# Keys and values turned in 64-row tiles, multiplied in 32-column tiles, and bias additions shared with ScalarE

## What is computed

```python
# L0: shifted windows of 8 x 8 pixels, 16 heads of 16 channels, one 64 x 64 matrix and a bias per head
y = einsum('nhjd,hij->nhid', windows(x), w) + b[None, :, :, None]
# L1: linear attention over all 4096 pixels, 64 heads of 8 channels
qkv = einsum('bchw,oc->bohw', x, w_qkv)
y = grouped_1x1(depthwise_5x5(qkv))
q, k, v = relu(q), relu(k), pad(v, ones)      # 32 heads from qkv, 32 from y
vk  = einsum('bhdn,bhen->bhde', v, k)         # 9 x 8 for each head
out = einsum('bhde,bhen->bhdn', vk, q);  out = out[:-1] / (out[-1:] + 1e-15)
out = batchnorm(einsum('bchw,oc->bohw', out, w_proj))
```

## Time and profile before

| | |
|---|---|
| median of three runs | 3008.99 us (3006.94 to 3009.3) |
| the profiled execution | 3003.14 us, its span 3001.5 us |
| mixing, until about | 450 us |
| projections, until about | 1300 us |
| heads, until about | 2410 us |
| output | the rest |
| granted TensorE clock, mean | 0.978 of 2.4 GHz |
| busy TensorE / VectorE / ScalarE / GpSimd | 91 / 74 / 48 / 29% |

### The profile page before, as it was taken

One profiled execution on the slowest core, in us unless ns is written; L12 is line 12 of the kernel. 1 busy time (PEld: TensorE's weight loads), 2 busy tenths in 40 slices (PEclk: granted clock), 3 DMA queues, 4 the chain that ended last, 5 costly groups with the idle time before them and its releaser, 6 DMA issues. The chain is left out here.

```text
span 3001.5 us, 46675 instructions
## 1 busy us (share of the span) xinstructions
PE 2742.5 (91%) x14847; PEld 2197.1 (73%) x14847; DVE 2230.3 (74%) x3385; ACT 1449.6 (48%) x1977; POOL 864.8 (29%) x1109
## 2 busy tenths in 40 slices
PE   4999979999989999879999999999999969999997
PEld 3777768878877888757777777777777836666665
DVE  5787875445445544389999999999999957777674
ACT  3434425444544544456566566566656523333332
POOL 6300004444444444500000000000000027777776
PEclk9999989999999999989999999999999989999999
DMA  4535336765766675655545555555555456776662
GB/s 152 211 148 208 146 114 208 233 225 191 231 218 218 203 235 181 205 155 134 133 128 134 134 130 132 136 131 131 137 131 131 122 196 243 260 266 241 238 238 112
DMA packets 285057, 534.16 MB, mean 178 GB/s; under 512 B 35184, under 2 KB 232560, under 8 KB 279280
## 3 DMA queue, kind: packets, MB, share of 16 engines
q1 hardware_dynamic: 274256, 468.11, 50.7%
q0 software_dynamic: 7936, 38.80, 3.7%
q10 hardware_dynamic: 2720, 25.43, 2.3%
HBM read 281.26 MB, written 254.15 MB: 178 GB/s over the span
## 5 line engine op out<-in xcount | busy, mean ns | idle before, releaser
L1565 POOL TENSOR_TENSOR ql<-q,qh 128x1024 fp32r<-128x1024 f32 x128 | 304.1, 2399 | 1180.2 <-ACT qh L1593 1180.2
L1213 PE MATMUL c_ps<-dh,wh 128*128 128x512 f32 x1152 | 476.4, 414 | 87.5 <-ACT m2s L1132 66.9
L1213 PE MATMUL c_ps<-dh,wl 128*128 128x512 f32 x1152 | 454.8, 395 | 0.0
L1213 PE MATMUL c_ps<-dl,wh 128*128 128x512 f32 x1152 | 454.5, 395 | 0.0
L1125 ACT ACTIVATE dh<-diff 128x1088 fp32r<-128x1088 f32 x192 | 213.7, 1113 | 431.4 <-DVE diff L1329 430.5
L837 PE MATMUL o_ps<-xh,wqh 128*128 128x512 f32 x768 | 327.6, 427 | 40.6 <-DVE xl L914 30.9
L1213 PEld LDWEIGHTS c_ps<-dh,wh 128*128 128x128 f32 x1152 | 217.1, 188 | 153.2 <-issue 112.3
L837 PE MATMUL o_ps<-xl,wqh 128*128 128x512 f32 x768 | 306.5, 399 | 0.0
L837 PE MATMUL o_ps<-xh,wql 128*128 128x512 f32 x768 | 305.3, 398 | 0.0
L937 DVE COPY vT<-pt_ps 128x512 f32<-128x512 f32 x128 | 88.6, 692 | 247.7 <-PE pt_ps L851 247.7
L1329 DVE TENSOR_TENSOR diff<-raw 128x544 f32<-128x544 f32 x384 | 260.3, 719 | 7.8 <-DMA raw<-qkv_scratch 7.8
(11 more groups left out here) (201 smaller groups left out, 5753.4 us busy)
## 6 DMA issues: line engine op xcount, KB each, us to landing
qkv_scratch<-stage SPq DMA_DIRECT2D x384, 289.0 KB, 4.2
raw<-qkv_scratch SPq DMA_DIRECT2D x192, 578.0 KB, 5.0
qr_scratch<-qs SPq DMA_DIRECT2D x128, 256.0 KB, 3.1
yq_scratch<-qy SPq DMA_DIRECT2D x64, 512.0 KB, 5.5
q<-yq_scratch SPq DMA_DIRECT2D x128, 256.0 KB, 4.2
q<-qr_scratch SPq DMA_DIRECT2D x128, 256.0 KB, 5.1
ox<-x_scratch SPq DMA_DIRECT2D x8, 4096.0 KB, 15.5
out<-ox SPq DMA_DIRECT2D x8, 4096.0 KB, 12.6
```

Source lines behind the costliest of these rows:

```text
L1213: last = pe.matmul(c_ps[:, bank(hp, j, kind, m), :], w[hp][:, kind, part, o:o + P], cells[:, :, HALF * dy:HALF * dy + HALF * NB], start=(k ...
L1565: pool.tensor_tensor(parity_of(ql, n, tp), parity(n, tp), parity_of(qh, n, tp).bitcast(F32), ALU.subtract)\
```

## The change

Turned keys and values. Every block of 128 x 128 is turned by two transposes of 64 rows, one for each half of the partitions, each into a bank of its own, in the projections and in the heads. Products of keys and values are made in four pieces of 32 columns, each with the values of the same 32 channels and a column of ones, so the accumulator is 128 x 33 instead of 128 x 129; the mask has 32 columns too. The waits for a turn stand before the last matmul of the product ahead of it. In the heads one ScalarE instruction takes both banks. In the projections VectorE makes all four copies into `kv`, and ScalarE both copies of turned tiles.

Mixing. ScalarE adds the bias of pairs 1, 3, 5 and 7, one instruction a head, and normalises the next image in ten pieces: two before the third group's additions, two after each of its four. Before the first image VectorE waits for the constants, does all statistics and the scale, and then places the head matrices; ScalarE copies those after it has normalised.

```diff
+def turn_halves(pe, ident, ps, at, block):
+    for r in range(2):
+        rows = slice(HP * r, HP * r + HP)
+        last = pe.transpose(ps[:, r, HP * at:HP * at + HP], block[rows, :], ident[rows, rows])
+    return last
...
+            def add_bias_odd(b, g, par, hp):
+                n = (MIX_HEADS // 2) * g + hp
+                if hp == 1:
+                    at_least(act, k_full, N_K * b + 3 * WR * (g - 1))
+                act.wait_ge(m_full, N_M * b + n + 1)
+                for j in range(2):
+                    c0 = (2 * hp + j) * MIX_CH
+                    last = act.activation(yT[:, (g + par) % 2, :, c0:c0 + MIX_CH],
+                                          m_ps[:, n % 2, j * GP * MIX_CH:(j + 1) * GP * MIX_CH]
+                                          .rearrange("p (a c) -> p a c", c=MIX_CH),
+                                          ACT.Identity, bias=bias[:, 2 * hp + j:2 * hp + j + 1])
+                last.then_inc(m_taken_act, 1)
...
-                    at_least(pe, m_taken, N_M * b + n - 1)
+                    at_least(pe, (m_taken, m_taken_act)[hp % 2], N_M // 2 * b + n // 2)
...
# projections, ScalarE: for each of the two tiles u
                         def turned(u):
-                            act.activation(kT[:, u, :, :].rearrange("p a c -> p (a c)"), t_ps[:, 0, :], ACT.Relu)\
+                            act.activation(kT[:, u, :, :].rearrange("p a (r c) -> p r a c", r=2),
+                                           t_ps[:, :, 0:4 * HP].rearrange("p r (a c) -> p r a c", a=4), ACT.Relu)\
                                 .then_inc(k_turned, 1)
+                            act.activation(vT[:, u, :, :, :, 0:SQ].rearrange("p r a q c -> p r (a q) c"),
+                                           t_ps[:, :, 4 * HP:8 * HP].rearrange("p r (a c) -> p r a c", c=SQ), ACT.Copy)\
+                                .then_inc(v_turned, 1)
-                        key(0)
-                        key(1)
                         turned(0)
...
# projections, TensorE
                 for ct in range(CT):
                     for w, xx in ((wh, xh), (wl, xh), (wh, xl)):
+                        if k == 5 and ahead is not None:
+                            ahead()
...
                 for a in range(4):
-                    last = pe.matmul(vk_ps[:, u, 0:VW], kT[:, u, a, :], vT[:, u, a, :],
-                                     start=(n == 0 and a == 0), stop=(n == NCH - 1 and a == 3))
+                    for q in range(NSQ):
+                        ch = slice(SQ * q, SQ * q + SQ)
+                        last = pe.matmul(vk_ps[ch, u, 0:VS], kT[:, u, a, ch], vT[:, u, q // 2, a, q % 2, :],
+                                         start=(n == 0 and a == 0), stop=(n == NCH - 1 and a == 3))
...
# projections, VectorE
-                        for u in range(2):
-                            dve.wait_ge(o_full, o0 + 2 * u + 2)
...
+                        for j in range(4):
+                            dve.wait_ge(o_full, o0 + j + 1)
+                            dve.tensor_copy(kv[:, n % 2, j, :], o_ps[:, j % 3, :]).then_inc(kv_ready, 1)
...
# heads, TensorE: sum_vk in the same four pieces; in a step
-                    convolve(s, hp, j, 0)
+                    convolve(s, hp, j, 0, (lambda: v_ready(s - 1)) if prev else None)
                     if prev:
-                        turn_v(s - 1)
+                        turn(vy, vt_full)
...
-                    convolve(s, hp, j, 2)
-                    turn_k(s)
+                    convolve(s, hp, j, 2, lambda: k_ready(s))
+                    turn(ky, kt_full)
...
# heads, VectorE, keep_diagonal
-                dve.tensor_tensor(kept.rearrange("p (a b) n -> p a b n", a=2), prod[:, :, :, 0:P],
-                                  K["gmask"][:, :].unsqueeze(1).unsqueeze(1).broadcast_to([P, 2, 2, P]),
+                dve.tensor_tensor(kept.rearrange("p (a b) n -> p a b n", a=2), prod[:, :, :, 0:SQ],
+                                  K["sqmask"][:, :].unsqueeze(1).unsqueeze(1).broadcast_to([P, 2, 2, SQ]),
                                   ALU.mult).then_inc(diag_ready, 1)
```

More of the change, by code:

```diff
@@ L397, in body @@
                     b = 2 * i + par
[L398 to L406, removed]
-                    image, Tn, _, nsn = norm_of(b + 1)
-                    norm_std(act, image, Tn, nsn)
-                    if not (last_body and par == 1):
-                        normalise(b + 1, 1 - par)
+                    more = not (last_body and par == 1)
+                    fill(b, 0, par)
+                    fill(b, 1, par)
+                    for hp in (1, 3, 5, 7):
+                        add_bias_odd(b, 0, par, hp)
+                    fill(b, 2, par)
+                    image, Tn, _, nsn = norm_of(b + 1)
+                    for hp in (1, 3, 5, 7):
+                        add_bias_odd(b, 1, par, hp)
+                        if hp == 3:
+                            norm_std(act, image, Tn, nsn)
+                    if more:
+                        start_normal(b + 1)
+                        pieces = normal_pieces(b + 1, 1 - par)
+                        next(pieces)
+                        next(pieces)
+                    for hp in (1, 3, 5, 7):
+                        add_bias_odd(b, 2, par, hp)
+                        if more:
+                            next(pieces)
+                            last = next(pieces)
+                    if more:
+                        end_normal(b + 1, last)
             over_image_pairs(act, body)
@@ L417, in _ @@
             pe.transpose(k_ps[:, 0, 0:MIX_HEADS], b_wide[:, :], K["ident"][0:MIX_HEADS, 0:MIX_HEADS]).then_inc(b_turned, 1)
+            for link in norm_group_sums(pe, 0, T, mv, stat_ps, K["gavg"], ns):
+                link()
             pe.wait_ge(w_zero, 3)
@@ L1162, in body @@
                         high(s, 2, odd)
-                        for pair in range(2):
-                            take_v(s - 1, pair)
+                        take_v(s - 1)
                     middle(s, 1, bank(hp, j, 1, 0), 1 - odd)
@@ L1172, in body @@
                         weights_high(h + 1, 1 - hp)
-                    for pair in range(2):
-                        take_k(s, pair)
+                    take_k(s)
             over_head_pairs(act, body)
             s = AH * STEPS - 1
-            for pair in range(2):
-                take_v(s, pair)
+            take_v(s)
             act.wait_ge(pr_turned, 1)
@@ L1193, in _, with convolve @@
             pe.wait_ge(init, 1)
-            def convolve(s, hp, j, kind):
+            def convolve(s, hp, j, kind, ahead=None):
                 u = 3 * s + kind
@@ L1242, in sum_vk @@
                         a = 2 * b + half
-                        last = pe.matmul(vk_ps[:, pair, VW * b:VW * b + VW], kT[:, pair, a, :], vT[:, pair, a, :],
-                                         start=(half == 0), stop=(half == 1))
+                        for q in range(NSQ):
+                            ch = slice(SQ * q, SQ * q + SQ)
+                            last = pe.matmul(vk_ps[ch, pair, VS * b:VS * b + VS], kT[:, pair, a, ch], vT[:, q // 2, 4 * pair + a, q % 2, :],
+                                             start=(half == 0), stop=(half == 1))
                 last.then_inc(vk_full, 1)
```

199 lines of the change are left out of this document (104 added, 95 removed).

## The result

| | before | after |
|---|---|---|
| median of the runs | 3008.88 us (3006.27 to 3009.3) | 3022.78 us (3020.54 to 3025.85) |
| ratio, 95% interval | | 1.005 (1.0035 to 1.0065) |
| span of the profiled execution | 3001.5 us | 3019.6 us |
| first turn of the mixing | 45.91 | 42.57 |
| first turn of keys and values, projections | 450.39 | 439.04 |

The kernel became slower by half a per cent; faster by 51.5 us was forecast. From mark to mark the difference of the two spans, 18.1 us, is: start -3.3, mixing -8.0, projections +27.6, heads -1.6, their end +3.4, output 0.1. **The heads stage, which was to give 66 us, gave 1.6.**

The account below looks back on a forecast made before the run. VectorE was taken to bound the heads, TensorE the projections and mostly the mixing. Terms -66 + 36 - 17 - 4.5 = -51.5 us took the profiled 3003.1 us to 2951.6, a median of 2957 us; range 2905 to 3030.

Parts of the forecast that it names:

- Heads, -66 forecast: Heads stage: VectorE's shorter diagonal multiply and reduction save 1.07 us in each of 64 steps, 69 us, taken as 66.
- Rival C: Heads stage gives back half through a hidden wait of VectorE on TensorE or ScalarE: 33 us less, 2990; chance 0.1.
- ScalarE at nothing: Heads: ScalarE's merging of two copies of 512 into one of 1024 costs nothing, being busy 182 of 300 us.
- Projections, +36 forecast: Projections: added copies lengthen the ScalarE and VectorE chain, which becomes the bound; 33 us over 8 images, taken as 36.
- Rival B: Projections: the longer chain doesn't bind, so the 36 us become -5, total 2916 us; chance 0.12.
- Tiles: TensorE, heads and projections: small tiles run side by side; a four-tile set takes 0.05 us, a heads product 1.2.
- Mixing, -17 forecast: Mixing: moving half of VectorE's bias additions to ScalarE removes half of TensorE's 32 us of waits plus a little.
- Start, -4.5 forecast: Start: statistics run through after GpSimd's constants and weight copies move behind normalising, so the first turn comes 4.5 us sooner.
- The lower end of the range: Whole kernel: 2905 us, given as Rival B with the mixing at its best.
- the sign: Whole kernel: the change makes it faster, by 51.5 us; chance of faster 0.78, same 0.04, slower 0.18.

Follow-up runs that it names:

- a_swap: Changed kernel; in the heads ScalarE copies the first value product (`m2s`) ahead of the high half of the next key's differences: 2947.39 us, ratio 0.9787.
- b_swap: Kernel before, with only ScalarE's order in the heads changed (`m2s` ahead of the high half of the next key's differences): 3005.53 us, ratio 0.9993.
- the two extra multiplies: Changed kernel plus one unneeded VectorE multiply of 512 elements per heads step: beside the diagonal 3022.68 us; behind the joining of the queries 3060.11 us.
- a_load: Changed kernel; the third load of each image from the third on leaves out 20 of its 24 rows: 3016.48 us, ratio 1.003.
- a_order: Changed kernel; in the projections VectorE copies the first key and value ahead of the next chunk's low halves: 2963.64 us, ratio 0.9853.
- p_mix: Kernel before with only the new mixing and start: 2999.78 us, ratio 0.9965.
- p_proj: Kernel before with only the new projections: 3028.72 us, ratio 1.0064.

## Why the prediction was wrong

- **Heads, -66 forecast, -1.6 measured: the step that failed.** "64 x 1.07 = 69 us if TensorE keeps under the new 16.4 us" made only TensorE the possible next limit. TensorE did keep under it: 12.55 us and the measured turns and product (twice 0.84, and 0.89) make 15.1. The saving was right (VectorE's busy time fell by 1.1 us a step, 298.13 to 278.88 in the stretch), but a VectorE without idle time was taken for a VectorE that is the bound in every place. It is one link in a loop with ScalarE, and the shortened instructions stood just where VectorE filled the time until ScalarE answered. *a_swap*, *b_swap* and the two extra multiplies show it. The row to ask for was in the trace of before: ScalarE at 1501.46, with `m2s` ending at 1502.04, one handover ahead of the instruction after the diagonal. Rival C named this wait, but gave it half of the gain and a chance of 0.1; its price comes from that row: 0.2 us from the end of `m2s` to `vy`, all of it handover, so nothing was left of the gain.
- **ScalarE at nothing.** Its share, 182 of 300 us, said nothing of when it answers. In that place it was the last to answer, before and after: `vy` starts 0.20 us behind the end of `m2s` in both. In *b_swap*, where `m2s` is ready earlier, `vy` starts 0.08 us before the recorded end of the reduction, in the kernel before 0.02 us after it.
- **Projections, +36 forecast, +27.6 measured.** The mechanism was right, to the wait named: 8.38 us for 8.2 between the turns, and 4.21 for 4.44, since a product there costs about 0.6 us (4.21 less 0.84 and twice 1.38) rather than 0.8. Some 2 us of the 27.6 are the piece of before, which was short in that execution (857.0 us against 859.0 to 859.5 in three others). Taken alone the part costs 19 us by the medians and 22 or more by the traces. Rival B is out.
- **Tiles.** The overlap that the earlier trace rows suggest holds down to 33 columns: a set of four tiles takes about 36 ns, where 50 were taken. Products were estimated a little dear.
- **Mixing, -17 forecast, -8.0 measured.** The term was mis-sized. TensorE's waits for the drains of `m_ps` fell by 10 us, not 16, since ScalarE's own additions now come late too. Its idle time ahead of turning back (`k_ps`) rose from 8.4 to 12.8 us, 5.8 of it for the same additions. And with shorter periods the statistics wait longer for their loads, 18.8 us in all instead of 7.5, part of which *a_load* gave back.
- **Start, -4.5 forecast, -3.3 measured.** ScalarE's first normalising ran from 30.6 to 40.3 us and its four weight copies to 42.5, the first turn 0.1 us behind them. What the forecast left out is a table load of ScalarE, 1.28 us: before, it ran at 33.82 while VectorE had not finished the variance; now it starts at 27.85, behind the variance, and the chain waits for it.
- **End of the heads, not in the sum: +3.4.** Between the last turn of keys and the output stage TensorE waits a good deal, and the granted clock falls to its lower level, 1.2 GHz, for a part of the time (0.50 of 2.4 GHz from 2440 to 2450 us): it averages 0.745 from 2410 to 2490 us, against 0.827 from 2392 to 2470 before. The time of this piece goes with its granted clock, whichever code it has: 60.4 us before and 59.1 in *a_order* (the changed code), both at 0.77 in the mean of the piece; 63.1 and 62.6 in *p_mix* and *p_proj* (the old code) at 0.73; 63.8 in this execution at 0.68. So it isn't put down to the change.
- **The lower end of the range.** Rival B with the mixing at its best, -40, comes to 2893 us, not 2905. Nothing hung on it.

The range held the time; the sign was wrong. What came true is nearest to C, but with all of the gain gone instead of half, and with the projections' cost on top. That the time lies in the range is no credit to the sum: heads, mixing and start together gave 75 us less than forecast, and only the projections came out cheaper.

## What to carry to other kernels

- An engine without idle time in a stretch need not be the bound at every point in it. Before pricing a shorter instruction, look up what the *next* instruction on that engine needs, and when that was ready in the trace of before: the distance from there, less a handover, is the most that can be gained. Here it was 0.2 us, all of it handover, for two instructions shortened by 1.1 together.
- When a cover goes, the repair is often an order: the small answer that someone waits for ahead of the large work that nobody waits for yet. Two such moves turned +0.5% into -4%, and were worth nothing, or a third of a per cent, without the change.
- An extra instruction beside the shortened one and the same one elsewhere tell slack from bound, in two runs.

## What the runs showed of the hardware

The turns and the tiled products by shape, all 64 steps of the heads and all of the projections:

```profile
L90 PE MATMUL pt_ps<-ident,kv 64*128 64x64 f32 x2048 | 91.3, 229 | 0.0
L1297 PE MATMUL yvk_ps<-yvT,ykT 128*32 128x33 f32 x4096 | 49.3, 199 | 1.2 <-issue 1.2
```

The 64 matmul instructions of one step's tiled products (32 products of fp32 operands, two records each) took 0.77 us from the first start to the last result. Less the 0.20 of the last one, the starts lie within 0.57 us, 9 ns apart on average. The 16 turns of 64 rows by 64 columns took 0.71 us, less 0.23: 32 ns apart. The Trainium skill (TensorE: Matmul & The Clock Gate, Part 1) gives about 25 ns as the least distance between starts, which would be 1.6 us for the 64; this trace doesn't agree for tiles, which run side by side.

Going into the tiled form costs 0.09 to 0.10 us beyond the ordinary distance of 0.23, at both kinds of group; the untiled groups of the kernel before started 0.23 behind their predecessor. With three such groups in a heads step and four in a chunk, that is 0.3 and 0.4 us. Coming out isn't priced by these runs. The first two ordinary matmuls behind a tiled group start 0.31 to 0.33 us apart, but they did so behind the untiled groups of before too (0.32 and 0.31). From the last tiled start to the first ordinary one it is 0.15 to 0.16 us, and how much of that is coming out isn't shown. The prediction weighed against the change that, by the Trainium skill (TensorEngine Tiling (Array Packing), Key Properties), a change of tiling mode drains TensorE. The trace agrees that there is a price, and it didn't decide.
